# A two-layer transformer kernel: the router in late slots, q0/k0 and the shared products in other slots, four token buffers, and a layer's gate pairs behind the maxima of their slots

## The reference, cut to what matters

```
xn = layernorm(x)
x = x + attention0(xn) + fp4_ffn(xn)      # gate, up and down products on values rounded to FP4 in blocks of 16
xn = layernorm(x)
x = x + attention1(xn) + moe(xn)

moe: logits = relu(xn @ Wr1 + br1) @ Wr2 + br2           # the router, 8 experts
     the two largest of softmax(logits), weighted again by a softmax
     out = silu(xn @ Ws1 + bs1) @ Ws2 + bs2              # the shared expert, for every token
     plus the weighted results of the two chosen experts
```

## Time and profile before

| | |
|---|---|
| median of three runs | 1332.75 us (1329.68 to 1333.38) |
| profiled execution, own time | 1326.96 us |
| its span from first to last instruction | 1325.1 us |
| mean granted TensorE clock | 0.952 |
| busy: TensorE, VectorE, ScalarE, GpSimd | 83%, 69%, 61%, 39% of the span |

### The profile page before, as it was taken

One profiled execution on the slowest core, in us unless ns is written; L12 is line 12 of the kernel. 1 busy time (PEld: TensorE's weight loads), 2 busy tenths in 40 slices (PEclk: granted clock), 3 DMA queues, 4 the chain that ended last, 5 costly groups with the idle time before them and its releaser, 6 DMA issues.

```text
span 1325.1 us, 19383 instructions
## 1 busy us (share of the span) xinstructions
PE 1102.7 (83%) x6711; PEld 498.8 (38%) x6711; DVE 919.5 (69%) x1555; ACT 802.8 (61%) x1079; POOL 511.4 (39%) x514
## 2 busy tenths in 40 slices
PE   2678688888998898888888988898889866899995
PEld 1213323323432343234323432343234335788841
DVE  7878577877778877877788868786876222555633
ACT  1255376676776767676767676757676762333364
POOL 8641364244434443344335432541232241344420
PEclk9779789999999999999999999999999887999987
DMA  5622066116411741163127313611331256666763
GB/s 139 157 65 55 18 169 170 37 33 183 133 38 37 188 124 37 54 182 113 37 76 183 90 37 100 188 53 37 110 75 35 72 158 189 171 203 195 216 175 100
DMA packets 149633, 146.73 MB, mean 111 GB/s; under 512 B 13696, under 2 KB 142016, under 8 KB 149536
## 3 DMA queue, kind: packets, MB, share of 16 engines
q1 hardware_dynamic: 144048, 135.58, 37.2%
q0 software_dynamic: 4544, 9.38, 2.1%
q10 hardware_dynamic: 944, 0.54, 0.2%
HBM read 92.80 MB, written 52.12 MB: 109 GB/s over the span
## 4 chain that ended last, share of the span: by engine, by line
PE 41%; ACT 18%; DVE 17%; issue 7%; DVEq 5%; SPq 4%; DMA 3%; POOL 2%; ACTq 0%; POOLq 0%
DVE nm L1060 10%; ACT ex L772 9%; PE sums L393 8%; PE mx L405 7%; PE mx L490 5%; PE mx L499 5%; PE mx L374 5%; ACT L748 4%; PE ring L295 2%; PE ring L305 2%; PE ring L474 2%; SPq L1652 2%; DVEq L1010 1%; DMA scratch<-parts 1%; DMA rest<-parts 1%
## 5 line engine op out<-in xcount | busy, mean ns | idle before, releaser
L1060 DVE TENSOR_REDUCE nm<-mx 128x2 f32<-128x1024 f32 x512 | 601.1, 1216 | 102.4 <-PE mx L374 100.9
L772 ACT ACTIVATE ex<-mx 128x1024 f32<-128x1024 f32 x512 | 510.7, 1024 | 262.7 <-PE mx L405 262.4
L405 PE MATMUL mx<-qs,ks 128*128 128x512 bf16 (+1 forms) x1024 | 299.0, 391 | 37.1 <-ACT ex L772 11.3
L393 PE MATMUL sums<-ex,vs 128*18 128x512 f32 x2048 | 283.0, 612 | 4.4 <-ACT ex L772 1.7
L374 PE MATMUL mx<-km,qm 32*128 32x512 bf16 x1024 | 152.0, 397 | 63.4 <-DVE nm L1060 31.4
L405 PEld LDWEIGHTS mx<-qs,ks 128*128 128x128 bf16 (+1 forms) x1024 | 77.0, 98 | 308.9 <-ACT ex L772 129.8
L1500 POOL TENSOR_SCALAR binade<-binade 128x704 f32<-128x704 f32 (+1 forms) x24 | 57.0, 2376 | 251.7 <-DVE binade L1011 251.7
L374 PEld LDWEIGHTS mx<-km,qm 32*128 32x128 bf16 x1024 | 39.0, 91 | 216.5 <-issue 75.6
L1537 POOL DMA_INDIRECT xsort<-xn,pos_i x64 | 62.7, 979 | 76.6 <-DVE pos_i L1132 59.4
L1453 POOL TENSOR_TENSOR rstd<-veps,minus_half 128x4 f32<-128x4 f32 x16 | 16.7, 1046 | 182.9 <-DVE veps L970 182.9
L748 ACT ACT_TABLE_LOAD x64 | 82.1, 1283 | 1.2
(11 more groups left out here) (218 smaller groups left out, 1549.1 us busy)
## 6 DMA issues: line engine op xcount, KB each, us to landing
scratch<-parts SPq DMA_DIRECT2D x128, 256.0 KB, 3.7
ks<-scratch SPq DMA_DIRECT2D x64, 256.0 KB
qs<-scratch SPq DMA_DIRECT2D x64, 256.0 KB
qs<-wmoe SPq DMA_DIRECT2D x20, 578.0 KB, 4.0
ks<-wmoe SPq DMA_DIRECT2D x19, 578.0 KB, 3.8
qm<-scratch SPq DMA_DIRECT2D x64, 128.0 KB, 2.6
km<-scratch SPq DMA_DIRECT2D x64, 128.0 KB, 2.6
rest<-parts SPq DMA_DIRECT2D x32, 128.0 KB
```

What stands on the lines that cost most here:

```text
L393: done = pe.matmul(acc[32 * j:32 * j + 2 * VW, :], values[:, start:start + 2 * VW], ex[:, s % NEX, j, :], start=q == 0 and t == 0, stop=q ...
L405: done = pe.matmul(bank[:, j, :], ks[l][r, h, t * P:(t + 1) * P], qs[l][r, h, :], start=True, stop=True)
L772: act.activation(ex[:, s % NEX, 2 * i:2 * i + 2, :], bank[:, :, :], ACT.Exp, scale=SCALE).then_inc(free, 1)
L1060: dve.tensor_reduce(nm[l][:, t, h:h + 2], bank[:, :, :], AX.X, ALU.max, negate=True).then_inc(free, 1)
```

## The change

1. Router: `router_hidden` and `router_logits` of a batch go from A(b+1), slots 1d and 3d, to B(b), slots 12a and 13a; `router_sort` from 3d to 13a of B, and `router_exp` to 14b of B. `router_choice` goes to A slot 1m, `gate_difference` to 6m, `ranks` to 8a, `places` and `router_tanh` to 8b, `router_weights` to 10m. Turn B(7) keeps its own places.
2. `norm0` goes from slot 0b to 0a. `q0` and `k0` go from 2a and 3a to 4d and 6d (A(1): from 5a and 6a to 5d and 7d).
3. The two `shared_hidden` pairs go from 7b and 8b to 2d and 3d of A, `v1` from 8d to 1d. The steps of `quantize_h(b, 1)` go from 1m, 2m, 2c and 5m to 2m, 2c, 3m and 3c.
4. The two gate pairs of the next batch in turn B go from 6b and 7b to 6d and 7d.
5. GpSimd: `router_hits` comes first in each round, and `second_part` and `third_part` of the next batch come behind `round_h(b, 1)`.
6. Tokens have four buffers (`NX`). The queue of SyncE fetches tokens up to tile 4 and the weights of tile 4 ahead of `store_early` of the last batch; tokens and weights of tiles 5 and 6 between `load_max` and `store_late` (before: those of tile 4 alone).

```diff
-NW, NRES = 4, 4
+NW, NX, NRES = 4, 4, 4
...
-                pe.wait_ge(xg_in[i % 2], (i // 2 + 1) * 16)
+                pe.wait_ge(xg_in[i % NX], (i // NX + 1) * 16)
...
# TensorE (ScalarE and VectorE alike)
-                    if at == (0, "b"):
+                    if at == (0, "a"):
                         norm0(b + 1)
-                    if at == (2 if b > 1 else 5, "a"):
+                    if at == (4 if b > 1 else 5, "d"):
                         q0(b + 1)
-                    if at == (3 if b > 1 else 6, "a"):
+                    if at == (6 if b > 1 else 7, "d"):
                         k0(b + 1)
...
-                    if at == (8, "d"):
+                    if at == (1, "d"):
                         v1(b - 1)
                     if b - 1 < LAST:
-                        if at == (1, "d"):
-                            router_hidden(b - 1)
-                        if at == (3, "d"):
-                            router_logits(b - 1)
-                        if at == (10, "a"):
+                        if at == (8, "a"):
                             ranks(b - 1)
-                    if at == (7, "b"):
+                    if at == (2, "d"):
                         shared_hidden(b - 1, 0)
-                    if at == (8, "b"):
+                    if at == (3, "d"):
                         shared_hidden(b - 1, 1)
...
-                    if at == (6, "b"):
+                    if at == (6, "d"):
                         gate_pair(b + 1, 0)
-                    if at == (7, "b"):
+                    if at == (7, "d"):
                         gate_pair(b + 1, 1)
...
+                    if at == (12, "a"):
+                        router_hidden(b)
+                    if at == (13, "a"):
+                        router_logits(b)
...
# ScalarE
+                    if at == (14, "b"):
+                        router_exp(b)
...
# VectorE
-                    if at == (1, "m"):
+                    if at == (2, "m"):
                         quantize_h(b, 1, 0)
-                    if at == (2, "m"):
+                    if at == (2, "c"):
                         quantize_h(b, 1, 1)
-                    if at == (2, "c"):
+                    if at == (3, "m"):
                         quantize_h(b, 1, 2)
-                    if at == (5, "m"):
+                    if at == (3, "c"):
                         quantize_h(b, 1, 3)
...
-                        if at == (3, "d"):
-                            router_sort(b - 1)
-                        if at == (7, "m"):
+                        if at == (1, "m"):
                             router_choice(b - 1)
-                        if at == (7, "c"):
+                        if at == (6, "m"):
                             gate_difference(b - 1)
-                        if at == (10, "b"):
+                        if at == (8, "b"):
                             places(b - 1)
-                        if at == (11, "m"):
+                        if at == (10, "m"):
                             router_weights(b - 1)
...
+                    if at == (13, "a"):
+                        router_sort(b)
...
# GpSimd
-                if 1 < b < LAST:
+                if b >= 1:
+                    router_hits(b - 1)
+                round_h(b, 1)
+                if 1 <= b < LAST:
                     second_part(b + 1)
                     third_part(0, b + 1)
-                round_h(b, 1)
-                if b == 1:
-                    second_part(2)
-                    third_part(0, 2)
                 if b >= 1:
-                    router_hits(b - 1)
                     scatter(b - 1)
...
# SyncE
-                    for i in range(2, AHEAD):
+                    for i in range(2, NX + 1):
                         fetch_tokens(i)
+                    fetch_weights(NW)
                 store_early(1, b)
                 load_max(1, b)
                 if b == LAST:
-                    fetch_tokens(AHEAD)
-                    fetch_weights(AHEAD)
+                    for i in (1, 2):
+                        fetch_tokens(NX + i)
+                        fetch_weights(NW + i)
                 store_late(1, b)
```

More of the change, by code:

```diff
@@ L181, in two_layers @@
         wbuf = [spare[i // 2][:, i % 2 * WROW:(i % 2 + 1) * WROW] for i in range(NW)]
-        xg = [spare[i][:, 2 * WROW:2 * WROW + 2 * XW].rearrange("p (h c) -> p h c", c=XW) for i in range(2)]
-        xgT = [spare[i][:, 2 * WROW + 2 * XW:2 * WROW + 2 * XW + 2 * P] for i in range(2)]
-        yo = [spare[i][:, 2 * WROW + 2 * XW + 2 * P:2 * WROW + 2 * XW + 4 * P] for i in range(2)]
+        xg = [spare[i // 2][:, 2 * WROW + i % 2 * 2 * XW:2 * WROW + (i % 2 + 1) * 2 * XW].rearrange("p (h c) -> p h c", c=XW) for i in range(NX)]
+        behind_x = 2 * WROW + 4 * XW
+        xgT = [spare[i][:, behind_x:behind_x + 2 * P] for i in range(2)]
+        yo = [spare[i][:, behind_x + 2 * P:behind_x + 4 * P] for i in range(2)]
         hm = [work[:, 0:EC * TS].rearrange("p (c t) -> p c t", c=EC),
               h_sb[:, :, :].rearrange("p t f -> p (t f)")[:, 0:EC * TS].rearrange("p (c t) -> p c t", c=EC)]
-        over_tiles = [spare[i][:, 2 * WROW + 2 * XW + 4 * P:2 * WROW + 2 * XW + 4 * P + NTILE * E].rearrange("p (i e) -> p i e", e=E)
+        over_tiles = [spare[i][:, behind_x + 4 * P:behind_x + 4 * P + NTILE * E].rearrange("p (i e) -> p i e", e=E)
                       for i in range(2)]
@@ L227, in two_layers @@
         w_in = [sem(f"w_in{i}") for i in range(NW)]
-        xg_in = [sem(f"xg_in{i}") for i in range(2)]
+        xg_in = [sem(f"xg_in{i}") for i in range(NX)]
         y_out = [sem("y_out0"), sem("y_out1")]
@@ L478, in tile_in @@
             def tile_in(i):
-                pe.wait_ge(xg_in[i % 2], (i // 2 + 1) * 16)
+                pe.wait_ge(xg_in[i % NX], (i // NX + 1) * 16)
                 bank = to_ring(("T", i))
                 for h in range(2):
-                    done = pe.transpose(bank[:, h * P:(h + 1) * P], xg[i % 2][:, h, 0:P], ident[:, :])
+                    done = pe.transpose(bank[:, h * P:(h + 1) * P], xg[i % NX][:, h, 0:P], ident[:, :])
                 done.then_inc(ring_full, 1)
@@ L829, in work_a @@
                     if b - 1 < LAST:
-                        if at == (1, "d"):
-                            router_hidden(b - 1)
-                        if at == (4, "b"):
-                            router_exp(b - 1)
-                        if at == (9, "b"):
+                        if at == (8, "b"):
                             router_tanh(b - 1)
-                    if at == (7, "b"):
+                    if at == (2, "d"):
                         shared_hidden(b - 1, 0)
-                    if at == (8, "b"):
+                    if at == (3, "d"):
                         shared_hidden(b - 1, 1)
@@ L1684, in fetch_tokens @@
                 first = sp.value_load(x_row[0:1, i:i + 1], min_val=0, max_val=ROWS - TS)
-                if i >= 2:
-                    sp.wait_ge(ring_full, ring.at(("T", i - 2))[1] + 1)
-                    sp.wait_ge(y_row_ready, i - 1)
-                sp.dma_start(xg[i % 2], xsort[bass.ds(first, TS), :].rearrange("(h p) c -> p h c", p=P)).then_inc(xg_in[i % 2], 16)
+                if i >= NX:
+                    sp.wait_ge(ring_full, ring.at(("T", i - NX))[1] + 1)
+                    sp.wait_ge(y_row_ready, i - NX + 1)
+                sp.dma_start(xg[i % NX], xsort[bass.ds(first, TS), :].rearrange("(h p) c -> p h c", p=P)).then_inc(xg_in[i % NX], 16)
             def store_base(b):
@@ L1785, in _ @@
                 load_stacks(1, b, 0)
-            for i in range(AHEAD + 1, NTILE):
+            for i in range(NX + 3, NTILE):
                 if i == AHEAD + 4:
```

19 lines of the change are left out of this document (10 added, 9 removed).

## The result

The changed kernel took 1350.17 us (median of four runs, 1346.48 to 1352.02) against 1331.42 (1329.68 to 1333.38) beside it: a ratio of 1.013, 95% interval 1.0103 to 1.0157, 18.8 us slower. The forecast was 1330.4, with a range of 1319 to 1339. The profiled execution took 1348.47 (span 1346.7) against 1326.96, 21.5 more. That is 2.8 more than the medians say, because the profiled execution of the kernel before lies 4.5 under its median and this one 1.7 under its own.

| part | forecast | measured |
|---|---|---|
| start to A(1), with B(0) | +3.4 | +8.0 |
| A(1) | 0 | -0.1 |
| B(1) to B(6) | +7.8 | +15.9 |
| A(2) to A(6) | -3.2 | +2.4 |
| A(7) | 0 | +2.2 |

What follows compares the result with a forecast made beforehand. ScalarE's timeline was taken to show slots bound by two loops, table-load slots by ScalarE, and tiles by TensorE. Terms -3.2 + 7.8 + 3.4 - 10.4 = -2.4 gave 1330.4 us from 1332.75, range 1319 to 1339.

Steps and rivals of the forecast that it cites:

- A(2) to A(6): Attention turns A: shared pairs cost more, other slots gain; -3.2 us over five turns, bounds -8 and +3.
- Shared pairs at "d": A's slots 2 and 3: the fill of 1.88 waits for the second exponential; 6.75 us a slot against a mean of 6.19.
- Gate pairs at "d": B(1) to B(6): the pair waits for its slot's second exponential; slot 5.72 instead of 5.52, +0.4 us a turn.
- The router in B(1) to B(6): Slots 12 to 14: products hidden, the sort of 0.90 not; +0.9 us a turn, bounds +0.3 and +2.0.
- The rival that logits come late: B's slot 13: logits 1.2 late hold VectorE's maxima, then scores; +7.2, giving +4.8 in all, 1337.5 us; chance 0.20.
- The router in B(0): Before A(1): router products and Relu stand ahead of the first scores; +3.4 us, bounds +1 and +4.
- The tiles: Last tiles: tile 8 starts 3.5 earlier and 6.9 is gone behind it; -10.4 us, bounds -6 and -17.
- the third rival's case: Tiles: the token buffers do nothing, tile 8 starts as before; +1.1 in all, 1334 us; no separate chance given.
- GpSimd and SyncE in the turns: Turns: GpSimd's later second_part and SyncE's load_rows still finish in time, covered with about 7 us; cost 0.
- The first rival: Gate and shared pairs at "d" are filled before Silu could start, so free; -12.3 in all, 1320.5 us; chance 0.38.
- the Trainium skill's rule named in the prediction: ScalarE's table switches: about 2.66 us each, so pairs at "d" would cost nothing; the trace has 1.42.
- two fifths of it: Share of the free-pairs gain said to suffice, with the forecast's gains elsewhere, to be faster by over 0.3%.

Runs made afterwards that it cites:

- warm: The changed kernel with idle bf16 matmuls in TensorE's waits of slots 2 and 3 of A: 1342.72 us, ratio 1.0082 to the kernel before.
- shared_b: The changed kernel with the shared pairs at place b of slots 2 and 3 instead of d: 1327.45 us, ratio 0.997 to the kernel before.
- le_late: shared_b with the sort's last subtraction moved to slot 0 of the next A, its exponential to slot 2: 1326.43 us, ratio 0.9952.
- router_alone: The kernel before with only the change's router part, GpSimd's router_hits first: 1335.4 us, ratio 1.0028.
- tokens_alone: The kernel before with only the four token buffers and the new order of fetches: 1328.97 us, ratio 0.9971.
- stores_first: shared_b with SyncE's store_late and load_stacks ahead of the weights of tiles 6 and 7, tokens 6 and 7 before them: 1321.99 us, ratio 0.9924.
- qk_early: shared_b with q0 at place a of slot 3 and k0 at d of slot 4 in A(2) to A(6): 1326.05 us, ratio 0.994.
- pairs_b: shared_b with the gate pairs back at place b of slots 6 and 7: 1326.47 us, ratio 0.9949.

## Why the prediction was wrong, step by step

- **Shared pairs at "d"**, "1.94 + 1.88 + 0.25 = 4.07, and 2.67": right at 2.4 GHz (4.01 and 2.69; 6.70 and 6.68 a slot). The step that failed is its 1.88. That price was taken from a place where the fill lies ahead of the maxima, and supposed to hold behind two waits. Seven of the fourteen fills took 2.92 to 3.68, and at "d" nothing lies between a late fill and ScalarE. warm shows that this is the clock, 9.5 us, and shared_b that it is the place that exposes it. Without the late fills A(2) to A(6) stand at -3.5 (A(3), with none, has slots 0 to 11 in 49.5 where 49.4 was forecast), beside the forecast's -3.2.
- **Gate pairs at "d"**: 5.72 and 5.64 for 5.72. Right, but for a late fill in B(1) and B(5), 1.8 together.
- **The router in B(1) to B(6)**: "+0.9 a turn" was +1.6. The place, that VectorE has no slack there, was right; the term was mis-sized, because the 0.90 came from the earlier trace rows, where the subtraction took 0.19. Beside GpSimd's TENSOR_TENSOR it takes 0.95 (le_late shows that 1.0 of the slot goes with it); 0.90 with 0.95 for the 0.19 is 1.66. The trace of the kernel before had such rows in three turns, at 0.92 to 1.17. In B(1) and B(5) slot 14 took 1.5 and 0.9 more still, TensorE being at the lower clock. The rival that logits come late did not occur: the bank was full when VectorE came to it.
- **The router in B(0)**: "+3.4". The chain was right but for one link: `router_exp` stands ahead of A(1)'s first exponential in ScalarE's list and waits for VectorE's sort (2.16 us, at 173.40 above). In shared_b and router_alone, where k1's product ran at the higher clock, the first exponential comes 4.31 after ScalarE has read k1, where it came 0.33 after before: +4.0, at the forecast's bound. The +8.0 of this execution holds 1.9 that was late before k1's product (A(0) has its slot of 4.59, as tokens_alone has too, so it isn't the change), 2.2 more for k1 and the up pair at the lower clock (2.07 and 2.55 for 1.12 and 1.35), 3.45 from the hidden product to the first score (168.89 to 172.34), and 0.5 more from the scores to the exponential. Over the traces the step costs 4.7.
- **The tiles**: "-10.4" was -6.8. Tile 4 without a wait, waits at tiles 5, 7 and 8, and 5.45 us of `clear_behind` after tile 7's weights came as described. What failed is the landing: "without them I take 2.8" was 4.7 (issued 1111.90, VectorE goes on at 1116.63). The stores alone aren't the reason for the 7.1 before either: in stores_first they leave 1.5 behind the scatter, and it lands after 4.83. In the kernel before they left 0.8 ahead of it; whether that order makes the 7.1 is not shown. With an issue 1.2 later, `store_late` came 75.3 after B(7)'s start, 2.8 later than forecast, and tile 8 began 0.7 earlier, not 3.5. That is the third rival's case. The -6.9 behind tile 8 was near: tile 13 gained 7.1 in all, 6.4 of it behind tile 8.
- **GpSimd and SyncE in the turns**: the cost was 0 as forecast; slots 0 to 5 of B are as long as before.
- **The first rival**, pairs at "d" for nothing, fell: Silu waited for the fill in thirteen of the fourteen shared pairs (0.56 us at 2.4 GHz in A(4); only slot 2 of A(1) had no wait). By the Trainium skill's rule named in the prediction they would have been free; the measured switch, 1.42, decides here too. The rival's condition, "two fifths of it", was also too strict: with the forecast's -2.4, a sixth of the 9.9 that it adds would have made over 4 us.

Of the 24.0 us between the forecast's -2.4 and the +21.6 of this execution's span, 9.5 are shared fills at the lower clock in A, 4.2 lower clock in B(1) and B(5), 3.8 the mis-sized sort (1.93 a turn with the gates, where 1.3 was forecast), 4.6 the start up to A(1) and 3.6 the tiles; 1.7 went the other way. The largest term alone doesn't bring the median into the range: 1350.2 less 9.5 is 1340.7, still over 1339.

What stays open: why TensorE's clock falls ahead of one fill and not of the next. The 8 us ahead of A(5)'s first fill and of A(6)'s show the same work (6.72 and 6.68 busy). That filling the waits kept the clock up at these fills is shown (fourteen of fourteen, against seven of fourteen); what decides in between is not, and in warm it fell at other places instead.

## What to carry to other kernels

Before a product is moved behind the last wait of a slot, price it at the lower clock level too: where it had slack, its length didn't matter, and there both levels come through in full. A short VectorE operation priced in one slot must be priced again in the slot it goes to, by what GpSimd runs there. Read that price from every occurrence in the trace, not from one row: here one turn said 0.19 and another 1.17. In a queue that is worked off in order, look for the entry that waits for something late (here the weights of tile 6) and let what nobody holds go first: that was worth 5.5 us by the medians, as against some 4 for the two more buffers with their fetches.

## What the runs showed of the hardware

- **VectorE waits for GpSimd.** The subtraction began at 568.19 and ended at 569.14; GpSimd's first TENSOR_TENSOR ended at 569.08 (the row of two, whose members took 1992 and 1667 ns). In B(2) to B(6) it was the same each time (0.94 to 0.95). The reductions, which read PSUM, took 1.2 each beside the same operations. Not every operation of GpSimd does this: beside its TENSOR_SCALAR the subtraction took 0.19, in B(0) (at 173.18, GpSimd busy from 171.79 to 174.90) and in the earlier trace rows (at 578.49, GpSimd busy from 577.33 to 578.84). The Trainium skill, "SBUF — State Buffer", section "SBUF: two separate sides", says that the two engines share a pair of ports, locked for a whole instruction, and that a VectorE operation with two SBUF inputs needs it. For GpSimd's TENSOR_TENSOR the trace agrees (0.95, ending with it); for its TENSOR_SCALAR, which reads SBUF too, it does not (0.19), and there the measurement decides.
- **The clock falls in the turns, and a small change of order moves where.** The records show the lower level 5 times from A(1) to B(7) before, 11 times after, 3 in shared_b, 7 in warm and 1 in qk_early. A fall cost 0.5 in slot 8 of B (pairs_b), 0.9 to 1.5 in slot 14, and 0.8 to 1.7 at a pair at "d". The Trainium skill, "TensorE: Matmul & The Clock Gate", section "A second HAM failure mode: psum-queue depth-cycling", tells of a kernel whose short waits between groups of matmuls made its clock swing between the two levels. The fills here, each behind a wait of 0.52 for a bank, are in line with it, and so is warm, where filling the waits kept the clock up at the fills; but half of the fills did not fall with the same waits, and no run here shows why.
- **The same code starts A(1) at 165.5 in one execution and at 170.1 in another** (before and tokens_alone), through one slot of A(0) (3.09 or 4.59) and B(0). An effect of 3 us there can't be read from one profile.
